# Two small changes in a two-layer graph network kernel on one core: how the weighted one-hot is written, and how the low half of the sums is placed

## The reference, cut to what matters

```python
# layer 1
msg = h[src] @ W_msg.T + b_msg + edge_embed[type]
messages = segment_sum(msg, dst)
x = layernorm(x + gru(messages, x))
# layer 2
proj = x @ fc_weight.T
el, er = proj[src], proj[dst]
e = sum(leaky_relu(el + er, 0.2) * a, -1)
gate = sigmoid(sum(el * er, -1))
w = sigmoid(e * gate)
neigh = segment_sum(x[src] * w[:, None], dst) / max(deg, 1)[:, None]
x = layernorm(x + (1 + eps) * x + neigh)
```

## Time and profile before

| | |
|---|---|
| median of 3 runs | 2963.24 us (2961.48 to 2964.84) |
| profiled execution | 2978.43 us, of which 2976.6 us are the span |
| TensorE busy | 1959.1 us (66%) |
| VectorE busy | 2691.1 us (90%) |
| ScalarE busy | 1571.2 us (53%) |
| GpSimd busy | 2108.7 us (71%) |
| layer 1's counts and sums | up to about 725 us |
| layer 2's loop | 850 to 2935 us |

### The profile page before, as it was taken

The page is one execution under the profiler, slowest core; times in us unless marked ns, Lnnn a source line. Parts: engine busy times, 40 slices in busy tenths (PEclk is TensorE's granted clock), DMA queues, the critical chain, the costliest instruction groups (busy, mean ns, idle before and its releaser), DMA issues. The chain is left out here.

```text
span 2976.6 us, 63843 instructions
## 1 busy us (share of the span) xinstructions
PE 1959.1 (66%) x13872; PEld 1688.4 (57%) x13872; DVE 2691.1 (90%) x13389; ACT 1571.2 (53%) x3622; POOL 2108.7 (71%) x2219
## 2 busy tenths in 40 slices
PE   6999999999945555555555555555555555555554
PEld 3888888887534455444444544544445544544543
DVE  8998998996889999999999989999999999999997
ACT  5877777775544444444444444444444444444445
POOL 2476777766667777777777777777777777777771
PEclk9999999999966766767677677666676676676765
DMA  8233333333354444444444444444444444444442
GB/s 210 61 99 96 98 96 94 100 91 104 106 170 135 135 135 132 139 135 135 135 133 135 138 138 135 131 135 139 137 135 135 135 136 139 135 135 135 139 136 69
DMA packets 241191, 376.21 MB, mean 126 GB/s; under 512 B 109269, under 2 KB 157612, under 8 KB 240428
## 3 DMA queue, kind: packets, MB, share of 16 engines
q0 software_dynamic: 99456, 271.71, 30.9%
q1 hardware_dynamic: 139380, 102.20, 12.3%
q10 hardware_dynamic: 2212, 0.60, 0.1%
HBM read 350.21 MB, written 23.61 MB: 126 GB/s over the span
## 5 line engine op out<-in xcount | busy, mean ns | idle before, releaser
L1619 POOL DMA_INDIRECT got<-rows,idx x1624 | 1564.3, 963 | 506.4 <-issue 477.3
L1824 PE MATMUL sum_ps<-whot,got 128*128 128x128 f32 x3264 | 694.7, 383 | 530.4 <-DVE whot L1631 430.3
L1824 PEld LDWEIGHTS sum_ps<-whot,got 128*128 128x128 f32 x3264 | 599.9, 275 | 609.1 <-DVE whot L1631 483.4
L1817 PE MATMUL er_ps<-win,hot_t 128*128 128x128 bf16 x4932 | 506.1, 277 | 401.2 <-ACT hot_t L1764 379.7
L1817 PEld LDWEIGHTS er_ps<-win,hot_t 128*128 128x128 bf16 x4932 | 450.7, 130 | 450.2 <-ACT hot_t L1764 415.7
L1631 DVE TENSOR_SCALAR whot<-iota_f,dl,w_s 128x128 f32<-128x128 f32 x1632 | 457.8, 362 | 158.7 <-ACT w_s L1769 158.6
L842 POOL DMA_INDIRECT got<-y_rows,idx x448 | 456.9, 1020 | 200.2 <-issue 134.0
L1000 ACT CAST cols<-c_ps 128x318 fp32r<-128x318 f32 x1176 | 493.5, 440 | 144.9 <-PE c_ps L1086 107.0
L1032 PE MATMUL span_ps<-y_parts,cols 128*126 128x256 f32 x2968 | 568.4, 319 | 0.2 <-ACT cols L1000 0.2
L1760 ACT ACTIVATE apart<-dst_b,less 128x512 bf16<-128x512 int16 x406 | 290.0, 714 | 342.3 <-DMA dst_b<-dst_row 336.5
L1032 PEld LDWEIGHTS span_ps<-y_parts,cols 128*126 128x126 f32 x2968 | 453.6, 192 | 5.5 <-issue 1.3
(11 more groups left out here) (256 smaller groups left out, 1829.5 us busy)
## 6 DMA issues: line engine op xcount, KB each, us to landing
dst_b<-dst_row SPq DMA_DIRECT2D x59, 512.0 KB
got<-rows,idx POOLq DMA_INDIRECT x1624
dst_b<-dst_row SPq DMA_DIRECT2D x59, 384.0 KB
win<-parts SPq DMA_DIRECT2D x118, 96.0 KB, 3.7
got<-y_rows,idx POOLq DMA_INDIRECT x448
parts<-split SPq DMA_DIRECT2D x12, 384.0 KB, 3.5
y_rows<-y_parts SPq DMA_DIRECT2D x1, 3584.0 KB, 9.9
rows<-nodes SPq DMA_DIRECT2D x12, 256.0 KB, 2.3
```

Source lines behind the costliest of these rows:

```text
L1619: pool.indirect_dma_start(got[:, c, i, :], None, rows, bass.IndirectOffsetOnAxis(ap=idx1[:, c, i:i + 1], axis=0)).then_inc(gathered[c], 16)
L1817: mm = pe.matmul(er_ps[:, c, i * D:(i + 1) * D], hot_t[:, c, i * P:(i + 1) * P], win[:, int(c >= HALF), part, :], start=(part == 0), stop= ...
L1824: mm = pe.matmul(sum_ps[:, 0:P], got[:, c, i, D:2 * D], whot[:, c, i, :], start=(c == 0 and i == 0), stop=(c == NS - 1 and i == STEP - 1))
```

## The change

In layer 2, `weigh` uses `scalar_tensor_tensor` in place of `tensor_scalar`: `dl` stays a scalar for each partition, and the weight becomes a second tensor operand, one column broadcast to 128. In layer 1, `copy_sums` becomes two ScalarE copies of 128 columns, the second into a tile of type float32r, and `place` becomes float32r; the matmul of the high half reads `place` as float32 as before, and that of the low half has both operands in float32r, which is one pass.

```diff
-            turned_s = sb("turned_s", [P, 2, YW], F32, ph)
-            place = sb("place", [P, 2, P], F32, ph)
+            turned_s = sb("turned_s", [P, 2, D], F32, ph)
+            turned_lo = sb("turned_lo", [P, 2, D], F32R, ph)
+            place = sb("place", [P, 2, P], F32R, ph)
...
-                        act.copy(turned_s[0:ROWS, h, :], span_ps[0:ROWS, h, 0:YW]).then_inc(s_copied, 1)
+                        act.copy(turned_s[0:ROWS, h, :], span_ps[0:ROWS, h, 0:D])
+                        act.copy(turned_lo[0:ROWS, h, :], span_ps[0:ROWS, h, D:YW]).then_inc(s_copied, 1)
...
-                        for i in range(2):
-                            mm = pe.matmul(out_ps[:, 0:P], turned_s[0:ROWS, h, i * D:(i + 1) * D],
-                                           place[0:ROWS, h, :], start=(i == 0), stop=(i == 1))
-                        mm.then_inc(posted, 1)
+                        pe.matmul(out_ps[:, 0:P], turned_s[0:ROWS, h, :], place[0:ROWS, h, :].bitcast(F32),
+                                  start=True, stop=False)
+                        pe.matmul(out_ps[:, 0:P], turned_lo[0:ROWS, h, :], place[0:ROWS, h, :],
+                                  start=False, stop=True).then_inc(posted, 1)
...
-                            m = dve.tensor_scalar(whot[:, c, i, :], iota_f[:], dl[:, at:at + 1], w_s[:, c, i:i + 1],
-                                                  ALU.is_equal, ALU.mult)
+                            m = dve.scalar_tensor_tensor(out=whot[:, c, i, :], in0=iota_f[:], scalar=dl[:, at:at + 1],
+                                                         in1=w_s[:, c, i:i + 1].to_broadcast([P, P]),
+                                                         op0=ALU.is_equal, op1=ALU.mult)
```

## The result

The changed kernel takes 2974.18 us (median of 5 runs, 2972.79 to 2976.84) against 2964.84 for the kernel before beside it (5 runs, 2961.48 to 2969.93). The ratio is 1.0032, with an interval of 1.0017 to 1.0046. It is 9.3 us slower, where 24 us less were forecast.

A forecast was written before the change was run, and what follows sets the result against it. TensorE was taken to bound layer 1 and GpSimd's gathers layer 2's loop. Gathers -18 us and layer 1 -6 us make -24 us, from the runs' median 2963.2 to 2939 us; range 2928 to 2959.

The forecast's parts named there:

- What bounds the kernel: TensorE sets layer 1; layer 2's loop lasts as long as GpSimd's 1624 gathers, VectorE stalling 2.74 us a body.
- VectorE's length: Layer 2, `whot`: the new form takes as long as the old, term zero; the stall falls to about 2.4 us.
- What the form does to the gathers: Layer 2: the old `whot` holds up gathers sharing time with it, the new one ends that: -18 us, ends 0 and 28.
- Rival (a): Layer 2's gathers are held by something else, or two-input instructions hold them too: 2957 with layer 1's gain, 2963 without; chance 0.17.
- The size of what was to be had: Layer 2's loop: all unevenness of the gathers' steps is 28 us, the most the new form could gain.
- both alike: Whole kernel: the profiled execution is 15 us above the median of the runs, taken to shift both kernels equally.
- Layer 1: Layer 1, `post`: one float32r pass replaces two passes of 0.11 us in 56 runs, gaining 6.2 us on TensorE.
- The tail: End of layer 2: the 23 us after the last gather are VectorE's own and don't change.
- (b): Layer 2, `whot`: the broadcast operand lengthens each by more than 98 ns, VectorE becomes the bound: 3014 us; chance 0.08 with smaller kin.
- (c): Layer 2 pays and layer 1 doesn't, by a costly narrow float32r pass or a late second copy: 2945 us; chance 0.15.

The follow-up runs named there:

- ctl: The kernel before, with no edit, profiled a second time: 2971.47 us, ratio 1.0004 to the kernel before beside it.
- stt_er: Kernel before with `whot` by `scalar_tensor_tensor`, its second tensor 128 columns of `er_ps` in PSUM, the weights left out: 2965.46 us, ratio 0.9988 to the kernel before.
- score_after: The changed kernel, with `larger` written over `er_ps` in PSUM and the weighted sums (L1645) reading it there: 2967.50 us, ratio 1.0010 to the kernel before.
- score_l1: Kernel before with the layer 1 half of the change, old `whot`, and weighted sums (L1645) reading one input from PSUM: 2950.32 us, ratio 0.9953.
- l2_only: Kernel before with only the layer 2 half of the change, the new form of `whot`: 2999.61 us, ratio 1.0097 to the kernel before.
- score_ps: Kernel before with old `whot`; `larger` is written over `er_ps` in PSUM and the weighted sums (L1645) read it there: 2964.73 us, ratio 0.9985.
- free: Kernel before with the edits of `stt_er` and `score_ps` together, the weights left out: 2956.74 us, ratio 0.9961 to the kernel before.
- ts_odd: Kernel before with the old `tensor_scalar` form of `whot`, its rows made 129 columns long: 2970.85 us, ratio 1.0002 to the kernel before.

## Why the prediction was wrong, point by point

**What bounds the kernel: right.** GpSimd sets the loop, VectorE's stall before `whot` is a cover, and the time of the loop is the number of gathers times their mean. The 12 ns of the mean and the 17.7 us of the loop agree.

**VectorE's length: right.** The term was zero. Four `whot` take 1.12 to 1.13 us in both forms, and the stall is 2.6 us a body, against 2.4 forecast. The 67 ns more for each that I had estimated from the Trainium skill ("VectorE: DVE Perf Modes", The perf-mode tier table) aren't in this trace: the group's mean is 340 ns against 363.

**What the form does to the gathers: wrong, in sign.** This is the step that failed: the term of -18 us, that the old form of `whot` holds up the gathers and the new one ends it. Measured against `ctl` it was +17.7 us in the loop, 22.1 us held at `whot` instead of 3.4. I had counted the gathers that *share time* with `whot`, found them 28 ns long on the mean, and named the form of `whot` as the cause. Sharing time was the wrong measure. L1645 stands just ahead of `whot` on VectorE, so a gather that starts within L1645 runs on into `whot`. Sorted by start, that trace has 18.8 us at L1645 and 3.8 at `whot`, so even a form that held nothing would have given some 4 us, not 18. The rows that I rested it on show this when one line above them is read. In the kernel before:

```profile
2004.94 0.29 DVE L1645 CUSTOM_DVE_ANT_0 scratch<-scratch,a_all 128x128 f32<-128x128 f32 x1
...
1136.66 0.27 DVE L1645 CUSTOM_DVE_ANT_0 scratch<-scratch,a_all 128x128 f32<-128x128 f32 x1
```

The gather of 1.01 us in the earlier trace rows starts at 2005.05, 0.11 us after such an L1645. The gather of 1.90 us in the earlier trace rows starts at 1136.74, 0.08 us after the first of four. That it ended with `whot` proved nothing: in `stt_er` gathers of 1.77 us stand at L1645 alone. And the quick gather of 2008.86, which I took as proof that two SBUF inputs do no harm, had started 0.30 us *before* L1645. An instruction that starts more than 0.05 us later doesn't slow a gather that is under way: at most three of the some 950 gathers elsewhere in a trace take over 0.96 us. I had the culprit in hand and used it as the witness for the defence.

With its cause changed the term changes sign: the new form is of the kind that holds. It costs 17.2 us (`score_after` against `score_l1`), 29 in `l2_only`, and 14.5 in the change itself (1.0032 against 0.9983). Rival (a) was right that the two-input form holds a gather too, and wrong that this leaves things as they are: of the gathers that start at `whot` 63 of 383 take over 0.96 us in `ctl`, and 224 of 371 in the changed kernel. The Trainium skill's sentence ("SBUF — State Buffer", Who interferes with whom) that an instruction with two SBUF inputs contends with a GpSimd instruction that reads SBUF would have given the sign. `stt_er` and `score_ps` agree with it: with one input in PSUM, the gathers that start within the freed instruction take 0.94 to 0.96 us, but for those just ahead of the old `whot`.

**The size of what was to be had: too large.** The 28 us of unevenness were of one execution. `ctl` has 13.9 us, and `free` gains 12.7 us in the median. The 15 us between that profile and the median of the runs were not a shift "both alike", as I had put it. They were in large part the very unevenness that I meant to remove: 9 ns more for each of 1624 gathers than in `ctl` is 15 us.

**Layer 1: right, and a bit more than forecast.** The step with `post` in the changed kernel, TensorE and ScalarE in time order:

```profile
431.75 0.30 ACT L981 COPY turned_s<-span_ps 126x128 f32<-126x128 f32 x1
431.90 0.32 ACT L982 CAST turned_lo<-span_ps 126x128 fp32r<-126x128 f32 x1
...
432.49 0.31 PE L1088 MATMUL c_ps<-right,left 128*128 128x318 bf16 x1
...
432.99 0.39 PE L1047 MATMUL out_ps<-place,turned_s 126*128 126x128 f32 x2
433.13 0.31 PE L1049 MATMUL out_ps<-place,turned_lo 126*128 126x128 f32 x1
433.28 0.31 PE L1088 MATMUL c_ps<-right,left 128*128 128x318 bf16 x1
```

From 432.49 to 433.28 the step takes 0.79 us, against 0.94 and 0.83 forecast; the medians of all steps with `post` and three blocks of `span_ps` say the same (0.789 us in 45, 0.946 in 44 before). That is 0.15 us x 56 = 8.4 us, where I had 6.2. The last `c_ps` comes 8.3 us earlier than in the profile before (714.73 to 706.47). Three passes take 0.30 us of the step, where four took 0.45, so the one narrow float32r pass took less than one of the float32 passes. ScalarE's two copies start 0.15 us apart and end within 0.5 us; TensorE waits for the second one once in the whole run, for 0.8 us. In plain runs the half gives 5 us beside the old layer 2 and 9.5 beside `score_ps`.

**The tail: right.** 65.4 us after the last gather's start, against 65.2.

**Rivals (b) and (c)** didn't come: VectorE isn't the bound, and it is layer 1 that pays. One sum of the chances was off besides: rival (a) had 0.17 with "a bit over half" faster, but entered the chance of faster with 0.07.

## What to carry to other kernels

When instructions of two engines are suspected of holding each other up, sort them by where one *starts* within the other, and look at what stood ahead of it, before an overlap is put down to the neighbour with which most time is shared. Where GpSimd's gathers set the time, give each long VectorE instruction beside them at most one SBUF tensor, the other in PSUM; a `tensor_scalar` beside them still cost something here. A mean that is 1% above its median is worth comparing with a second execution before it is booked as gain.

## What the runs showed of the hardware

- A gather (an indirect DMA of 128 rows, 0.95 us on GpSimd) is held if it *starts* within a VectorE instruction with two SBUF tensor inputs. In `ctl`, with L1645 of 0.29 us, gathers that start 0.05, 0.08, 0.10, 0.12 and 0.14 us after it take 1.07, 1.03, 1.01, 0.98 and 0.97 us in the median: the later, the less. Start and lengthening add up to 0.15 to 0.17 us for nearly all, so the hold ends there, well ahead of the 0.29 us at which the instruction is listed to end. A few are held through the following ones as well. Starts of 0.00 to 0.03 us aren't held in `ctl`, and those after 0.15 us only where they lie just ahead of `whot` (below).
- With the new `whot`, most starts from 0.07 to 0.21 us after one of the four are held, over half the pitch of 0.26. Some are held through all that is left of the four, 1.7 to 1.8 us (21 gathers above 1.5 us in `l2_only`, two in the changed kernel). There are such long ones in the kernel before too (1762 ns in `ctl`, 1890 in the earlier trace rows), and none in `free` from 1220 to 2900 us.
- The old form, with one SBUF tensor and two scalars for each partition, holds less: in `ctl` starts 0.11 to 0.19 us after one of its instructions take 0.97 to 1.06 us, many of them, and of 36 starts 0.02 to 0.05 us ahead of the first of four 33 take 0.98 to 1.00. The first gather below starts 0.04 us ahead and is held, the second 0.10 us after it and isn't (`ctl`):

```profile
1420.11 0.99 POOL L1619 DMA_INDIRECT got<-rows,idx  x1 [0.30 <-issue]
1420.15 1.10 DVE L1631 TENSOR_SCALAR whot<-iota_f,dl,w_s 128x128 f32<-128x128 f32 x4
...
1401.22 1.13 DVE L1631 TENSOR_SCALAR whot<-iota_f,dl,w_s 128x128 f32<-128x128 f32 x4
1401.32 0.95 POOL L1619 DMA_INDIRECT got<-rows,idx  x1 [0.30 <-issue]
```

  Why the old form holds at all wasn't told apart, since `ts_odd` left it as it was.
- Moving one input to PSUM costs VectorE nothing here: 0.28 us against 0.29 for L1645, 1.12 us for four `whot`.
